# A two-pass sequence kernel whose Toeplitz halves are loaded ready-made instead of being split on chip

## The reference, cut to what matters

```python
# x: (128, 128, 2048) fp32, cond: 128 indices of 16 weight matrices, length: 128 sequence lengths
W = weights[cond]
x = x + einsum('bct,bcd->bdt', x, W)                 # first layer: a row product for each b
mask = arange(2048) < length[:, None]
dtA = (-exp(log_A_real) + 1j * A_imag) * exp(log_dt)[:, None]
Cs = C * (exp(dtA) - 1) / A
k = 2 * real(einsum('hn,hnl->hl', Cs, exp(dtA[:, :, None] * arange(2048))))
y = causal_convolution(x * mask, k) + x * mask * D   # second layer: one kernel k[h] for each channel h
return x + y * mask
```

## Time and profile before

| | |
|---|---|
| median of 3 runs | 2387.25 us (2386.72 to 2394.55) |
| profiled execution | 2383.36 us, its span 2381.3 us |
| PE, DVE, ACT, POOL busy | 2225.9, 2007.1, 1647.8, 1322.1 us |
| DMA | 648.07 MB, mean 272 GB/s |

### The profile page before, as it was taken

The page is one execution under the profiler, slowest core; times in us unless marked ns, Lnnn a source line. Parts: engine busy times, 40 slices in busy tenths (PEclk is TensorE's granted clock), DMA queues, the critical chain, the costliest instruction groups (busy, mean ns, idle before and its releaser), DMA issues.

```text
span 2381.3 us, 61811 instructions
## 1 busy us (share of the span) xinstructions
PE 2225.9 (93%) x15101; PEld 1934.9 (81%) x15101; DVE 2007.1 (84%) x4125; ACT 1647.8 (69%) x4864; POOL 1322.1 (56%) x1864
## 2 busy tenths in 40 slices
PE   5777776999999999999999999999999999999999
PEld 1222222988888889988898888899999999999999
DVE  4999300999999899999999899988888888888887
ACT  4444544778777777777777777766766666766766
POOL 0894500777777777777777777634334334334332
PEclk9999999999999999999999999999999999999999
DMA  8999899788888888888888888767777777777776
GB/s 299 361 353 364 339 353 353 260 294 287 297 287 291 290 293 295 300 287 294 299 292 287 286 289 296 252 209 213 218 217 214 216 216 216 216 217 215 216 217 189
DMA packets 278052, 648.07 MB, mean 272 GB/s; under 512 B 31362, under 2 KB 146308, under 8 KB 278020
## 3 DMA queue, kind: packets, MB, share of 16 engines
q1 hardware_dynamic: 259012, 578.49, 75.1%
q10 hardware_dynamic: 19008, 69.21, 7.2%
HBM read 328.82 MB, written 318.77 MB: 272 GB/s over the span
## 4 chain that ended last, share of the span: by engine, by line
PE 40%; POOL 31%; issue 18%; ACTq 5%; ACT 3%; DMA 2%; POOLq 1%; DVE 1%; SPq 0%; DVEq 0%
POOL x_lo L491 13%; PE bank L895 7%; PE bank L896 7%; PE bank L897 7%; POOL outer L466 6%; PE bank L864 6%; PE bank L937 5%; PE bank L877 5%; POOL e_mat L471 4%; POOL e_rev L473 4%; ACTq L523 4%; PE bank L929 4%; POOL w_lo L488 2%; POOL par L463 1%; ACT w_sel L524 1%
## 5 line engine op out<-in xcount | busy, mean ns | idle before, releaser
L789 DVE TENSOR_TENSOR u_lo<-bank,u_hi 128x512 fp32r<-128x512 f32 x512 | 350.0, 684 | 98.2 <-ACT u_hi L602 98.1
L463 POOL COPY par<-table 128x72 f32 (+1 forms) x256 | 104.2, 407 | 552.5 <-PE bank L897 489.8
L491 POOL TENSOR_TENSOR x_lo<-row_x,x_hi 128x256 fp32r<-128x256 f32 x496 | 395.8, 828 | 0.0
L937 PE MATMUL bank<-toep,u_odd 128*128 128x128 f32 x2048 | 394.7, 274 | 0.0
L864 PE MATMUL bank<-row_x,w_sel 128*128 128x512 f32 x528 | 275.0, 648 | 124.9 <-ACT w_sel L524 109.5
L548 ACT ACTIVATE row_y<-bank 128x512 f32<-128x512 f32 x512 | 304.0, 594 | 116.9 <-PE bank L864 116.4
L801 DVE COPY_PREDICATED decay<-mask,bank 128x512 f32<-128x512 uint8 x512 | 375.3, 733 | 0.8 <-PE bank L897 0.6
L611 ACT ACTIVATE state<-bank 128x128 f32<-128x128 f32 x768 | 214.6, 279 | 221.1 <-PE bank L929 122.7
L895 PE MATMUL bank<-t_hi,u_hi 128*128 128x256 f32 x1024 | 354.5, 346 | 9.7 <-DVE decay L801 9.7
L864 PEld LDWEIGHTS bank<-row_x,w_sel 128*128 128x128 f32 x528 | 94.5, 199 | 302.8 <-issue 164.8
L466 POOL TENSOR_TENSOR outer<-par 128x256 f32<-128x256 f32 x512 | 317.5, 641 | 20.5
(11 more groups left out here) (145 smaller groups left out, 5974.2 us busy)
## 6 DMA issues: line engine op xcount, KB each, us to landing
row_x<-in_x SPq DMA_DIRECT2D x256, 512.0 KB, 6.2
decay<-x_scratch SPq DMA_DIRECT2D x256, 512.0 KB, 5.6
out<-decay SPq DMA_DIRECT2D x256, 512.0 KB, 3.5
x_scratch<-row_y ACTq DMA_DIRECT2D x132, 512.0 KB, 5.9
x_scratch<-row_y SPq DMA_DIRECT2D x124, 512.0 KB, 3.6
toep<-k_scratch SPq DMA_DIRECT2D x256, 128.0 KB, 4.9
k_scratch<-k_pad SPq DMA_DIRECT2D x128, 192.0 KB, 4.8
b_scratch<-b_whole SPq DMA_DIRECT2D x128, 128.0 KB, 3.3
```

What stands on the lines that cost most here:

```text
L491: last = pool.tensor_tensor(x_lo[i][:, cols], row_x[j][:, cols], x_hi[i][:, cols].bitcast(fp32), ALU.subtract)
L789: v.tensor_tensor(u_lo[j % 2][:, blocks, :], t_bank[q][:, :].rearrange("s (k b) -> s k b", b=B), u_hi[j % 2][:, blocks, :].bitcast(fp32), ...
L937: mm(y[:, P:CHUNK], u_odd[i][:, c, :], toep[j][:, 0:P], start=False, stop=True, skip_group_check=True)
```

## The change

The diff goes through SP, POOL, ACT (row stage, then channels), DVE (`mats`, `keep_k`, channels) and PE in this order. Four edits. The kernel row is reversed and kept on 16 partitions only (`k_rows`, [whole, high, low] side by side); ACT and DVE halve this row (`halve_k`, `split_k`) and three DMAs for each channel load t_hi, t_lo and the odd blocks' `toep` ready; PE then reads t and e with reversed columns, e is made reversed at once and e_rev is gone. The matrices r and m are one product each of two 64-column halves; the row of C is split once in the set-up and read with a stride of 0; b is stored and loaded as its two halves. ACT issues the row stores of the first segment, where SP did, and SP issues the load of x1 ahead of the Toeplitz load. In the row stage `pick_w` runs two rows ahead instead of one.

```diff
-TOEP = P * (P + CHUNK)
+COPIES = 16
+KROW = P + CHUNK
...
+        halves = sb("halves", [P, N])
+        ck_all = sb("ck_all", [P, H, 2], fp32r)
+        ck = [sb(f"ck{i}", [P, 2], fp32r) for i in range(2)]
+        b_mat = [sb(f"b_mat{i}", [P, 2, 2, P], fp32r) for i in range(SLOTS)]
+        k_rows = [sb(f"k_rows{i}", [COPIES, 3, KROW]) for i in range(2)]
+        toep = [sb(f"toep{i}", [P, P]) for i in range(SLOTS)]
...
             def load_toeplitz(seg, k, j, gd):
-                skewed = k_dram[bass.ds(k - seg * H, 1), P:TOEP].rearrange("a (s w) -> (a s) w", w=P + CHUNK - 1)[:, 0:CHUNK]
-                sp.dma_start(toep[j][:, :], skewed).then_inc(toep_loaded[j], 16)
+                row = k_dram[bass.ds(k - seg * H, 1), 0:1, 0:1]
+                for n, dst, first in ((1, t_hi[j][:, :].bitcast(fp32), 0), (2, t_lo[j][:, :].bitcast(fp32), 0), (0, toep[j][:, :], P)):
+                    skewed = bass.AP(row.tensor, row.offset + (n * KROW + first), [[3 * KROW + P // COPIES, COPIES], [1, P // COPIES], [1, CHUNK - first]])
+                    sp.dma_start(dst, skewed).then_inc(toep_loaded[j], 16)
...
             def store_b(k, j):
-                sp.wait_ge(b_half, k + 1)
+                sp.wait_ge(b_ready, k + 1)
...
+                    if then:
+                        load_x1(then[0], then[1], j2, then[2])
                     if after and after[0] == 0:
                         load_toeplitz(0, k + 1, j1, after[2])
-                    if then:
-                        load_x1(then[0], then[1], j2, then[2])
...
-                    if with_rows:
-                        store_row(k + ROWS_FIRST, j, 1, k + AHEAD)
...
+                if seg == 0:
+                    pool.tensor_copy(ck[j % 2][:, :], ck_all[:, bass.ds(k, 1), :].rearrange("p a n -> p (a n)"))
...
-                pool.tensor_tensor(e_mat[j][:, :], outer[:, 0, :], outer[:, 1, :], ALU.add).then_inc(e_ready, 1)
-                if seg == 0:
-                    pool.tensor_tensor(e_rev[j % 2][:, :], outer[:, 0, CHUNK - 1::-1], outer[:, 1, CHUNK - 1::-1], ALU.add).then_inc(e_ready, 1)
+                pool.tensor_tensor(e_mat[j][:, :], outer[:, 0, CHUNK - 1::-1], outer[:, 1, CHUNK - 1::-1], ALU.add).then_inc(e_ready, 1)
...
-                            pick_w(n + 1, (j + 1) % SLOTS)
+                            pick_w(n + 2, (j + 2) % SLOTS)
...
+            def halve_k(k, j):
+                act.wait_ge(k_made, k + 1)
+                row = k_rows[j % 2]
+                nc.scalar.activation(row[:, 1, 0:CHUNK].bitcast(fp32r), row[:, 0, 0:CHUNK], ACT.Copy).then_inc(k_half, 1)
...
                     keep_s(seg, k, j, 2)
+                    if then and then[0] == 0:
+                        halve_k(k + 2, j2)
                     if after:
                         keep_u(k + 1, j1, 1)
                     keep_s(seg, k, j, 3)
+                    if then and then[0] == 0:
+                        keep_b(k + 2, j2)
                     if with_rows:
                         take_row(k + ROWS_FIRST, j, 0, row_bank)
                     if next_row:
                         halve_x(k + 1, j1, 1)
-                    if after:
-                        halve_toeplitz(j1, after[2])
-                    if then:
-                        keep_b(then[0], k + 2, j2)
...
                     if with_rows:
                         take_row(k + ROWS_FIRST, j, 1, row_bank)
+                        store_row(k + ROWS_FIRST, j, 1, k + AHEAD)
...
+                def pairs(dst, col):
+                    return v.tensor_tensor(dst[:, :].rearrange("p (a n) -> p a n", a=2), halves[:, :].unsqueeze(1).to_broadcast([P, 2, N]),
+                                           p[:, col:col + 2].unsqueeze(2).to_broadcast([P, 2, N]), ALU.mult)
+
+                pairs(r_mat[j], COL_R).then_inc(mats_ready, 1)
                 if seg == 0:
+                    pairs(m_mat[i], COL_M).then_inc(mats_ready, 1)
...
-                v.scalar_tensor_tensor(k_pad[i][:, P:P + CHUNK], delta, par[j][:, COL_DP:COL_DP + 1], k_part, ALU.mult, ALU.add).then_inc(k_ready, 1)
+                v.scalar_tensor_tensor(k_rows[i][:, 0, 0:CHUNK], delta[0:COPIES, CHUNK - 1::-1], par[j][0:COPIES, COL_DP:COL_DP + 1],
+                                       k_part[0:COPIES, :], ALU.mult, ALU.add).then_inc(k_made, 1)
+
+            def split_k(k, j):
+                row = k_rows[j % 2]
+                dve.wait_ge(k_half, k + 1)
+                v.tensor_tensor(row[:, 2, 0:CHUNK].bitcast(fp32r), row[:, 0, 0:CHUNK], row[:, 1, 0:CHUNK], ALU.subtract).then_inc(k_ready, 1)
...
                     split_s(seg, k, j, 2)
+                    if then and then[0] == 0:
+                        split_k(k + 2, j2)
                     if after:
                         split_u(k + 1, j1, 1)
                     split_s(seg, k, j, 3)
-                    if after:
-                        split_toeplitz(k + 1, j1)
                     take_y(seg, k, j, 0)
-                    if then:
-                        split_b(then[0], k + 2, j2)
+                    if then and then[0] == 0:
+                        split_b(k + 2, j2)
...
-                split_mm(k_part, ck_hi[i][:, :], ck_lo[i][:, :], e_hi[j][:, :], e_lo[j][:, :], start=True, stop=True)
+                split_mm(k_part, ck[i][:, 0:1].to_broadcast([P, P]), ck[i][:, 1:2].to_broadcast([P, P]), e_hi[j][:, :], e_lo[j][:, :], start=True, stop=True)
...
-                split_mm(y, u_hi[i][:, 2 * c, :], u_lo[i][:, 2 * c, :], t_hi[j][:, :], t_lo[j][:, :], start=(c % 2 == 0), stop=False)
-                mm(y[:, P:CHUNK], u_odd[i][:, c, :], toep[j][:, 0:P], start=False, stop=True, skip_group_check=True)
+                split_mm(y, u_hi[i][:, 2 * c, :], u_lo[i][:, 2 * c, :], t_hi[j][:, CHUNK - 1::-1], t_lo[j][:, CHUNK - 1::-1], start=(c % 2 == 0), stop=False)
+                mm(y[:, P:CHUNK], u_odd[i][:, c, :], toep[j][:, P - 1::-1], start=False, stop=True, skip_group_check=True)
...
-                    pe.wait_ge(toep_split, k + 1)
+                    pe.wait_ge(toep_loaded[j], k * 12 + (48 - j * 12))
```

More of the change, by code:

```diff
@@ L60 @@
 COL_P1, COL_P2, COL_Q1, COL_Q2 = 0, HIGH, 2 * HIGH, 2 * HIGH + LOW
[L61 to L62 removed]
+COL_M, COL_R, COL_DP = NTRIG, NTRIG + 2, NTRIG + 4
+NCOL = NTRIG + 5
 HS = 16
@@ L160, in s4d_program @@
         w_lo = [sb(f"w_lo{i}", [P, P], fp32r) for i in range(2)]
-        b_whole = [sb(f"b_whole{i}", [P, 2, P]) for i in range(2)]
         bank = [ctx.enter_context(nc.psum_tensor(f"bank{i}", [P, BANK], fp32)) for i in range(8)]
@@ L197, in s4d_program @@
         b_half = sem("b_half")
-        b_stored = [sem(f"b_stored{i}") for i in range(2)]
-        b_loaded = [sem(f"b_loaded{i}") for i in range(2)]
+        b_stored = [sem(f"b_stored{i}") for i in range(SLOTS)]
+        b_loaded = [sem(f"b_loaded{i}") for i in range(SLOTS)]
         b_ready = sem("b_ready")
@@ L421, in _ @@
             for i in range(2):
-                pool.memset(k_pad[i][:, 0:P], 0.0).then_inc(pads_zeroed, 1)
+                pool.memset(k_rows[i][:, :, CHUNK:KROW], 0.0).then_inc(pads_zeroed, 1)
             pool.iota(step_i, [[1, T]], base=0, channel_multiplier=0).then_inc(steps_made, 1)
@@ L548, in take_row, with store_row @@
                 nc.scalar.activation(row_y[j][:, q * BANK:(q + 1) * BANK], from_bank[:, :], ACT.Copy).then_inc(row_taken, 1)
+            def store_row(n, j, seg, b):
+                act.wait_ge(row_taken, n * NQ + NQ)
+                act.dma_start(x1_dram[seg][bass.ds(b, 1), 0:H * SEG].rearrange("a (h t) -> (a h) t", t=SEG), row_y[j][:, :]).then_inc(x1_stored[j], 16)
             def rows(g):
@@ L555, in rows @@
                         if q == 0:
[L556 to L559 removed]
+                            pick_w(n + 2, (j + 2) % SLOTS)
+                    if isinstance(g, int) and g >= GROUPS:
+                        store_row(n, j, 1, n - B)
+                    else:
+                        store_row(n, j, 0, n)
             def keep_parameters():
                 act.wait_ge(turned_done, 5)
[L563 removed]
+                for n, dst in enumerate((ar_t[:, :], f_t[:, :], table[:, :, COL_M], table[:, :, COL_M + 1])):
                     last = nc.scalar.activation(dst, bank[4][:, n * P:(n + 1) * P], ACT.Copy)
                 last.then_inc(turned_kept, 1)
[L566 removed]
+                nc.scalar.activation(ck_all[:, :, 0], bank[5][:, 0:P], ACT.Copy).then_inc(turned_kept, 1)
             def make_sines(half):
@@ L591, in first_matrices @@
                     halve_e(0, e, e)
-                keep_b(0, k, k)
+                halve_k(k, k)
+                keep_b(k, k)
             act.wait_ge(consts_in, 16 * (NSETUP + 1))
             pick_w(0, 0)
+            pick_w(1, 1)
             row_groups(act, rows, base_sines, keep_parameters, lambda: make_sines(0), lambda: make_sines(1), lambda: first_matrices(0), lambda: first_matrices(1))
@@ L619, in halve_edge @@
                 nc.scalar.activation(s_hi[0][:, :], edge[j % 2][:, :], ACT.Copy).then_inc(s_half, 1)
```

(18 more changed lines are left out.)

102 lines of the change are left out of this document (35 added, 67 removed).

## The result

The changed kernel takes 2445.29 us (median of 4 runs, 2443.32 to 2454.43) against 2387.19 us (4 runs, 2386.72 to 2394.55): 1.0243 times as long, interval 1.021 to 1.0277. The forecast was 2452 us, and slower. The profiled execution took 2447.23 us.

What follows compares the result with a forecast made beforehand. PE bounds the segments, with ACT almost without slack in the first; PE waits for w_sel in the row stage. 2383.4 + 93 - 25 - 3 = 2448 us, plus 3.9 for the median: 2452, own range 2405 to 2490, with rivals 2390 to 2500.

Steps and rivals of the forecast that it cites:

- The chain of the first segment: First segment: ACT's halve_k waits for DVE ahead of state 3; channel 9.70 us against 8.95, +93 us, from +56 to +124.
- The second loop, over POOL: First segment: x_hi 1, POOL's w_lo, par, matrices, halve_k, state 3 and back; 9.6 us, as long as the first loop.
- Rival 1: First segment: state 3's shift is absorbed and DVE's relief counts; channel 8.6 us, kernel 2316 us, chance 0.11.
- DMA in the first segment: Engines' 7.8 us a channel becomes 8.4 by bytes or 8.9 by descriptors, under the channel's 9.7 both times.
- The row stage: Row stage: picking the second row ahead takes pick_w off PE's chain; 2.76 us a row, -25 us, bounds 0 and -46.
- Rival 3: Row stage is held by DMA under the skill's 358 GB/s rule, nothing gained there; about 2473 us, chance 0.20.
- The second segment: Second segment: PE bounds it at 99.9% busy, channel keeps 6.4 us; -3 us, from -10 to +13.
- Rival 5: DMA binds the second segment: +0.1 us for each of 128 channels, kernel 2465 us, chance 0.05.
- reversed reads by PE: PE's matmuls with moving operands read backwards: no cost taken; at half speed +3.4 us a channel.
- the row store on ACT: First segment: store issue adds 0.15 + 0.34 us behind row_y 1, covered by ACT's idle time; uncovered it costs 61 us.
- x1 ahead of the Toeplitz load: SP's queue: it loses the wait on row_taken and issues x1 earlier; no cost was taken.

Runs made afterwards that it cites:

- The two kernels without the wait: Changed kernel with halve_k behind state 3 and split_k behind its low half, 2369.42 us; or with halve_k in place copying a constant, 2372.54 us.
- with 1472 KB: Changed kernel without the second segment's loads of t_lo and the odd blocks, five issues a channel: 2427.33 us, ratio 1.0178 to the kernel before.
- a kernel at 0.73: Changed kernel with Toeplitz matrix loaded whole, ahead of x1, and split on chip, b whole, rows stored by SP: 2392.88 us, 0.9918 of the kernel before.

## Why the prediction was right, step by step

**The chain of the first segment: right, in its places and nearly in its size.** Worked out were 2.60 us from state 1 to u_hi 0, 1.73 to `halve_k`, 1.05 to state 3, and 4.36 from there over PE to the next state 1 (0.28, 0.30, 2.13 and 1.65). The channel shown has 2.61, 1.72, 1.07 and 4.20: 9.60, against 9.74. The stretch after state 3 is the one that came out shorter. (From `drive` to state 1 the sum has 1.65 where its own rows give 1.70; measured are 1.59.) The growth was less than forecast, +0.59 us a channel for +0.75, also because the channel of before takes 9.00 us and not the 8.95 that it was given; that base was averaged over a window with the last, shorter channels. Terms under the sum were nearly right or were covered: the next instruction starts 0.33 us after the copy does, for 0.31; each matrix took 0.69 to 0.71 for 0.65, par 0.24 for 0.5. The two kernels without the wait show the cause, not only the sum. The second loop, over POOL, was given 9.6 as well; it wasn't the bound, since DVE idled 0.22 us between its matrices and u_lo, waiting for ACT. Its par was sized at twice what it took.

**Rival 1** said that the shift of state 3 would be absorbed: PE's 0.79 us a channel says no. Its other half, that a relieved DVE brings the channel to 8.6, was tested with the wait gone and did not hold either: 8.97 where DMA is at 0.98, 8.84 with fewer bytes.

**DMA in the first segment: nearly right.** I gave it 8.4 to 8.9 us a channel. The engines were busy 9.2 us of the changed channel (0.96 of 9.59) and 8.8 us with `halve_k` late (0.98 of 8.97), and 8.97 is the shortest channel seen with these bytes. DMA did not bind at 9.59, but it takes away what moving `halve_k` would otherwise bring.

**The row stage: right in kind, too small.** -42 for -25. ACT's list was taken at 2.70 us and DMA's limit at 412 GB/s over 16 us (2.55 us a row, for which the prediction has 2.52), and 2.76 was chosen above both; the stage now moves 398 GB/s over 350 us, 419 in its fullest stretch, at 2.64 us a row. Rival 3, the stage held at 354 GB/s, is thus wrong. The Trainium skill itself has the reason beside the rule: HBM Reference (Specifications (TRN2)) says that a core that streams alone measures about 425 GB/s and that the share of about 358 holds with both cores of a pair streaming. This kernel runs alone, and the trace agrees with 419.

**The second segment: the term that failed.** "PE bounds it at 99.9% busy with nothing to remove, so I take -3 us, from -10 to +13"; it was +31. I compared the DMA engines' sum with the channel (5.7 to 6.45 against 6.4) and took a full PE for a sign that nothing is late. The sum was the wrong measure: with few bytes the segment is as fast as before at a share of 0.71, with 1472 KB it has lost 11 us at 0.80, since x1 lands later while its issue hangs on the output store ahead of it. The bytes are shown as one cause of the late landing; a kernel at 0.73 that lands x1 as late shows that there is another, which stays open. Rival 5 put the loss down to full DMA engines, at two fifths of its size (+13 us) and a chance of 0.05; they were not full.

**At no cost, as forecast:** reversed reads by PE (1137.76 to 1137.88, both on reversed t: 0.12 us from start to start, the pitch that the prediction took), the row store on ACT, and x1 ahead of the Toeplitz load. The Trainium skill's note on 16-byte cachelines in SBUF — State Buffer, by which such reads are free, agrees with the 0.12 us. That the new order of loads is free was not tried alone in the changed kernel; its profile has hardly a wait for a Toeplitz half in the first segment (2.8 us, in 10 waits of the weight loads), and ACT, a link of the loop found above, no longer handles t_hi. The reason I gave, that SP's queue is relieved, does not name this, and in the kernel before the same two lines cost 10%.

**The number.** That the time came out within 0.3% is luck on top of a right mechanism: the errors are -17 us in the row stage, -18 in the first segment and +34 in the second, and cancel. The ends of the prediction's own terms, added up, give about 2394 to 2508 us, not the 2405 to 2490 that it names.

## What to carry to other kernels

Moving a split from two engines to DMA removes work where there was room and adds a handover and bytes where there was none: before adding a cross-engine wait, look which product of the same engine stands behind it and when its reader arrives; here `halve_k` two places later in the list is worth 2.6%. A load can be late long before the DMA engines are full, so look at issue, landing and need of the latest load at once, and not at the sum of bytes alone. Before swapping two loads in a queue, follow the queue round: if a store in it waits for an engine that waits for a load behind the store, whatever stands between can end up in the period.

## What the runs showed of the hardware

- Swapping a 512 KB and a 128 KB load in one queue moved the small one's landing from 3.9 to 6.2 us, and the kernel by 10%.
- Where waits left PE busy for 83% of a segment, its granted clock was 0.95 in the mean, with stretches at the lower level; at 92% (after the change) and 99% (before) it was 1.00.
- Operations on 16 partitions took as long as those on 128 with the same columns: 0.46 us for 16x256 on DVE against 0.47 for 128x256, and 0.42 us for `halve_k` on ACT, as for t_hi of 128x256 before.
- A matmul of 256 columns whose moving operand is read backwards started the next one after 0.12 us (1137.76 to 1137.88), and so did one whose weights are one column read 128 times (1133.10 to 1133.22 in the same channel); before the change it was 0.12 us as well (1132.45 to 1132.57).
- The DMA engines moved 398 GB/s in the row stage and, with `halve_k` late, 314 GB/s in the first segment, at a busy share of 1.00 and 0.98. A packet had 3596 bytes in the mean in the first and 2125 in the second; one of 4 KB took 159 ns, one of 1 KB 46 ns and one of 512 bytes 27 ns: smaller pieces, fewer bytes for the same busy time.
